# Gate and norm steps moved between VectorE, GpSimd and ScalarE, and the float16 half of the gelus moved to ScalarE, in a fused attention and expert kernel

## The reference

```python
# attention: 8 heads of 64, keys and values from the context and from x
x = x + tanh(g_xattn) * attention(layernorm(x), ctx, Wq1, Wk1, Wv1, Wk2, Wv2, Wo, bo)
# experts: 8 experts and a shared one, 128 -> 512 -> 128; two experts a token
logits = xf @ gate_w + gate_b
top_w, top_i = top_k(logits, 2)
gw = softmax(top_w)
combine = (gw[:, :, None] * one_hot(top_i, 8)).sum(axis=1)
for e in range(8):
    out += combine[:, e:e+1] * (gelu(xf @ w1[e] + b1[e]) @ w2[e] + b2[e])
shared = gelu(xf @ ws1 + bs1) @ ws2 + bs2
x = x + tanh(g_ffn) * (out + shared)
```

## Time and profile before

| | |
|---|---|
| median of 3 runs | 174.17 us (173.14 to 174.34) |
| profiled execution | 173.16 us |
| its span, first to last instruction | 171.0 us |
| mean granted clock of TensorE | 0.95 |
| busy: TensorE, VectorE, GpSimd, ScalarE | 144.5, 128.6, 123.9, 119.3 us |
| one undisturbed expert pass | 2.65 us |

### The profile page before, as it was taken

The page is one execution under the profiler, slowest core; times in us unless marked ns, Lnnn a source line. Parts: engine busy times, 40 slices in busy tenths (PEclk is TensorE's granted clock), DMA queues, the critical chain, the costliest instruction groups (busy, mean ns, idle before and its releaser), DMA issues.

```text
span 171.0 us, 4386 instructions
## 1 busy us (share of the span) xinstructions
PE 144.5 (84%) x1724; PEld 113.6 (66%) x1724; DVE 128.6 (75%) x267; ACT 119.3 (70%) x200; POOL 123.9 (72%) x98
## 2 busy tenths in 40 slices
PE   7789788568799989989997984999993599999973
PEld 4545334334578778767775873889992389999972
DVE  2779998647668868768698699877899955668681
ACT  3469663408989979889989896585964068787740
POOL 7639999619999999986879794836759355984430
PEclk9999999858999999999999997899999579999999
DMA  5599899970004701984000043000000000000002
GB/s 140 173 341 223 216 216 248 230 204 2 4 2 96 186 0 27 220 262 143 4 0 4 0 126 122 1 4 2 6 0 0 4 0 0 4 0 4 0 0 65
DMA packets 12925, 14.00 MB, mean 82 GB/s; under 512 B 1469, under 2 KB 9578, under 8 KB 12906
## 3 DMA queue, kind: packets, MB, share of 16 engines
q1 hardware_dynamic: 12906, 13.73, 30.4%
HBM read 7.18 MB, written 0.26 MB: 43 GB/s over the span
## 4 chain that ended last, share of the span: by engine, by line
PE 40%; DVE 30%; DMA 8%; POOL 6%; SPq 6%; issue 4%; ACT 3%; ACTq 0%; DVEq 0%
PE banks L951 8%; PE banks L952 8%; PE banks L953 8%; DVE nmax L783 4%; DVE v_lo L768 3%; DMA kab<-k_nat 3%; DMA ring<-in_L_ffn_w_dram 3%; PE banks L1051 2%; PE banks L1052 2%; SPq L452 2%; DVE wf L937 2%; PE banks L1032 2%; POOL p_lo L548 2%; DMA prob<-in_ctx_dram 2%; DVE kab L898 2%
## 5 line engine op out<-in xcount | busy, mean ns | idle before, releaser
L548 POOL TENSOR_TENSOR p_lo<-prob,p_hi 128x768 f16<-128x768 f32 x31 | 51.1, 1667 | 5.0 <-ACT p_hi L649 4.5
L783 DVE TENSOR_REDUCE nmax<-banks 128x1 f32<-128x768 f32 x32 | 30.5, 953 | 13.0 <-PE banks L1033 13.0
L587 POOL TENSOR_TENSOR kab<-kab 128x512 f16<-128x512 f32 x18 | 20.7, 1156 | 17.7 <-ACT kab L696 17.7
L641 ACT ACTIVATE prob<-banks 128x768 f32<-128x768 f32 x32 | 25.8, 805 | 9.1 <-PE banks L1052 8.1
L649 ACT ACTIVATE p_hi<-prob 128x768 f16<-128x768 f32 x32 | 27.0, 843 | 1.0
L690 ACT ACTIVATE kab<-banks,b1T 128x256 f32<-128x256 f32 x36 | 15.1, 471 | 17.5 <-PE banks L953 15.4
L951 PE MATMUL banks<-wf,kab 128*128 128x128 f16 x144 | 25.6, 222 | 1.0 <-DVE acc L929 0.9
L952 PE MATMUL banks<-wf,kab 128*128 128x128 f16 x144 | 25.6, 222 | 0.0
L953 PE MATMUL banks<-wf,kab 128*128 128x128 f16 x144 | 25.5, 222 | 0.0
L1052 PE MATMUL banks<-qab,kab 66*128 66x256 f16 x96 | 23.6, 278 | 0.0
L1051 PE MATMUL banks<-qab,kab 128*128 128x256 f16 x96 | 23.6, 278 | 0.0
(11 more groups left out here) (148 smaller groups left out, 392.1 us busy)
## 6 DMA issues: line engine op xcount, KB each, us to landing
ring<-in_L_ffn_w_dram SPq DMA_DIRECT2D x16, 256.0 KB, 3.9
kab<-k_nat SPq DMA_DIRECT2D x4, 384.0 KB, 4.6
kab<-k_nat SPq DMA_DIRECT2D x6, 192.0 KB, 4.5
kab<-k_nat SPq DMA_DIRECT2D x2, 576.0 KB, 7.1
qab<-qo SPq DMA_DIRECT2D x2, 384.0 KB, 6.3
kab<-k_nat SPq DMA_DIRECT2D x2, 288.0 KB, 8.0
prob<-in_ctx_dram SPq DMA_DIRECT2D x2, 256.0 KB, 4.7
ring<-in_L_xattn_Wk_dram SPq DMA_DIRECT2D x2, 256.0 KB, 4.2
```

The costliest lines, as they stand in the source:

```text
L548: nc.gpsimd.tensor_tensor(p_lo[:, j % 3, dst, :], prob(j, g)[:, 0:n, :], p_hi[:, j % 3, dst, :], ALU.subtract).then_inc(pl_done, 1)
L783: nc.vector.tensor_reduce(nmax[:, i, q:q + 1], span(0, KEYS), AX_X, ALU.max, negate=True).then_inc(max_done, 1)
```

## The change

There are four parts.

1. Norm: VectorE stops at mean and variance. GpSimd adds epsilon, takes the power, and makes -mean times rstd (`away`). ScalarE makes the normalised rows as one instruction of scale and bias a tile (`normal_rows`), in the step of TAIL_X; for batch 0 they stand between the two halves of the exponentials.
2. Gate: VectorE makes logits, largest values and marks, and the copy of the two largest is a reduction. GpSimd makes e to (logit - largest) for all eight experts, the mask and their product. VectorE sums it and takes the reciprocal. ScalarE multiplies (`combine`), as the last thing of its step.
3. Hidden chunks 2 and 3: their float16 copy goes from VectorE to ScalarE, behind the last gelu; both halves now count on `hh_act`.
4. Late weights: the low halves of experts 3 and 4 go from VectorE to GpSimd, and the steps are new for all of them. Also, VectorE makes the last `p_lo` at the start of its step.

```diff
-LO_BY_DVE = [3, 4]
-HI_STEP = {3: 13, 4: 14, 5: FFN0, 6: FFN0 + 3, 7: FFN0 + 6, 8: FFN0 + 9}
-LO_STEP = {3: 16, 4: 17, 5: FFN0 + 1, 6: FFN0 + 5, 7: FFN0 + 8, 8: FFN0 + 11}
+HI_STEP = {3: 13, 4: 14, 5: FFN0 + 1, 6: FFN0 + 4, 7: FFN0 + 7, 8: FFN0 + 10}
+SCALE_STEP = {3: FFN0, 4: FFN0 + 1, 5: FFN0 + 3, 6: FFN0 + 6, 7: FFN0 + 9, 8: FFN0 + 12}
+LO_STEP = {3: FFN0, 4: FFN0 + 2, 5: FFN0 + 4, 6: FFN0 + 7, 7: FFN0 + 10, 8: FFN0 + 13}
...
# GpSimd, in its steps
                         pool.wait_ge(var_ready, 2 + b)
-                        nc.gpsimd.tensor_tensor(rstd[:, t:t + QT], vare[:, t:t + QT], c_mhalf[:, t:t + QT],
-                                                ALU.pow).then_inc(rstd_ready, 1)
+                        link(nc.gpsimd.tensor_scalar(vare[:, t:t + QT], mv[:, t:t + QT, 1], EPS, None, ALU.add))
+                        link(nc.gpsimd.tensor_tensor(rstd[:, t:t + QT], vare[:, t:t + QT], c_mhalf[:, t:t + QT],
+                                                     ALU.pow))
+                        at = slice(QT * b, QT * b + QT)
+                        link(nc.gpsimd.tensor_scalar(away[:, 0, at], mv[:, t:t + QT, 0], -1.0, None, ALU.mult))
+                        nc.gpsimd.tensor_tensor(away[:, 1, at], away[:, 0, at], rstd[:, t:t + QT],
+                                                ALU.mult).then_inc(rstd_ready, 1)
                     if s == TAIL_GATE:
-                        pool.wait_ge(gexp_go, b + 1)
-                        nc.gpsimd.tensor_tensor(gexp[:, QT * b:QT * b + QT], c_e[:, :],
-                                                gdiff[:, QT * b:QT * b + QT], ALU.pow).then_inc(gexp_done, 1)
+                        at = slice(QT * b, QT * b + QT)
+                        pool.wait_ge(pick_done, b + 1)
+                        link(nc.gpsimd.tensor_tensor(gap[:, at, :], logit[:, at, 0:E],
+                                                     top8[:, at, 0:1].broadcast_to([P, QT, E]), ALU.subtract))
+                        link(nc.gpsimd.tensor_tensor(gap[:, at, :], c_e[:, :].unsqueeze(2).broadcast_to([P, QT, E]),
+                                                     gap[:, at, :], ALU.pow))
+                        link(nc.gpsimd.tensor_scalar(mask[:, at, :], marked[:, at, 0:E], PICKED, None, ALU.is_equal))
+                        nc.gpsimd.tensor_tensor(first[:, at, :], gap[:, at, :], mask[:, at, :],
+                                                ALU.mult).then_inc(gate_done, 1)
                 k = i - FFN0 - 1
                 if 0 <= k < NF:
-                    pool.wait_ge(hh_act, k + 1)
+                    pool.wait_ge(hh_act, 2 * k + 1)
...
                 for j in range(EARLY, NE):
-                    if j not in LO_BY_DVE and i == LO_STEP[j]:
+                    if i == SCALE_STEP[j]:
                         scale_late(j)
-                    if j not in LO_BY_DVE and i == LO_STEP[j] + 1:
+                    if i == LO_STEP[j]:
                         lo_late(j)
# ScalarE
+            def normal_rows(b):
+                act.wait_ge(rstd_ready, 2 + b)
+                for t in range(QT * b, QT * b + QT):
+                    nc.scalar.activation(xn[:, t, :], acc[:, t, :], ACT.Identity, bias=away[:, 1, t:t + 1],
+                                         scale=rstd[:, NT + t:NT + t + 1]).then_inc(xn_ready, 1)
+            def combine(b):
+                act.wait_ge(gate_sum, b + 1)
+                tiles = slice(QT * b, QT * b + QT)
+                for t in range(QT * b, QT * b + QT):
+                    nc.scalar.activation(comb[:, t, 0:E], first[:, t, :], ACT.Identity,
+                                         scale=gtop[:, t, 0:1]).then_inc(comb_part, 1)
+                act.wait_ge(comb_part, QT * (b + 1))
+                nc.scalar.activation(comb_s[:, tiles, :], comb[:, tiles, :], ACT.Identity,
+                                     scale=scales[:, 1:2]).then_inc(comb_ready, 1)
             for i in range(STEPS):
+                if i == TAIL_STEP[1][TAIL_X]:
+                    normal_rows(1)
...
+                if i == TAIL_STEP[0][TAIL_X]:
+                    normal_rows(0)
...
+                    act.wait_ge(gelu_done, HC * (k + 1))
+                    nc.scalar.activation(hid_hi[:, k % HB, HALF:], hid_b(k), ACT.Copy).then_inc(hh_act, 1)
+                for b in range(B):
+                    if i == TAIL_STEP[b][TAIL_COMB]:
+                        combine(b)
# VectorE, first in step 19 + k
-                    if k >= HB:
-                        dve.wait_ge(y_ps, k - HB + 1)
-                    dve.wait_ge(gelu_done, HC * (k + 1))
-                    nc.vector.tensor_copy(hid_hi[:, k % HB, HALF:], hid_b(k)).then_inc(hh_dve, 1)
-                    dve.wait_ge(hh_dve, k + 1)
+                    dve.wait_ge(hh_act, 2 * k + 2)
                     nc.vector.tensor_tensor(hid_lo[:, k % HB, HALF:], hid_b(k), hid_hi[:, k % HB, HALF:],
                                             ALU.subtract).then_inc(hl_dve, 1)
# VectorE, gate (TAIL_GATE, then TAIL_COMB); L855 to L864 and L809 to L819 are what goes
-                    mark(nc.vector.tensor_copy(pick8[:, tiles, 0:2], top8[:, tiles, 0:2]))
...
+                    link(nc.vector.tensor_reduce(pick8[:, tiles, 0:2], top8[:, tiles, 0:2].unsqueeze(3), AX_X, ALU.max))
...
+                    dve.wait_ge(gate_done, b + 1)
+                    link(nc.vector.tensor_reduce(gsum[:, tiles], first[:, tiles, :], AX_X, ALU.add))
+                    nc.vector.reciprocal(gtop[:, tiles, 0], gsum[:, tiles]).then_inc(gate_sum, 1)
# TensorE, before the hidden chunks of expert j for batch 0
-                        elif j in LO_BY_DVE:
-                            pe.wait_ge(f_lo_dve, LO_BY_DVE.index(j) + 1)
                         else:
-                            pe.wait_ge(f_lo_pool, j - EARLY - len(LO_BY_DVE) + 1)
+                            pe.wait_ge(f_lo, j - EARLY + 1)
```

More of the change, by code:

```diff
@@ L280, in block_kernel @@
         mask = sb("mask", [P, NT, E], F32)
+        gap = sb("gap", [P, NT, E], F32)
+        away = sb("away", [P, 2, NT], F32)
         first = sb("first", [P, NT, E], F32)
-        gdiff = sb("gdiff", [P, NT], F32)
-        gexp = sb("gexp", [P, NT], F32)
         gsum = sb("gsum", [P, NT], F32)
@@ L557, in lo_late @@
             def lo_late(j):
-                pool.wait_ge(f_scaled, j - EARLY + 1 - len(LO_BY_DVE))
+                pool.wait_ge(f_scaled, j - EARLY + 1)
                 hi, lo = [wf[:, a, EORDER[j], :, :].rearrange("p a n -> p (a n)") for a in range(2)]
                 nc.gpsimd.tensor_tensor(lo, ring_f(j).rearrange("p a n -> p (a n)"), hi,
-                                        ALU.subtract).then_inc(f_lo_pool, 1)
+                                        ALU.subtract).then_inc(f_lo, 1)
             for j in range(1, EARLY):
@@ L724, in row_statistics @@
                 for t in range(tiles):
-                    mark(nc.vector.bn_aggr(mv[:, first + t, :], stats[:, first + t, :]))
+                    last = nc.vector.bn_aggr(mv[:, first + t, :], stats[:, first + t, :])
+                    if first > 0 and t == tiles - 1:
+                        last.then_inc(var_ready, 1)
+                    else:
+                        mark(last)
                 settle()
+                if first > 0:
+                    return
                 nc.vector.tensor_scalar(vare[:, first:first + tiles], mv[:, first:first + tiles, 1], EPS, None,
@@ L803, in tail_first @@
                 tiles = slice(QT * b, QT * b + QT)
-                if s == TAIL_X:
-                    normalise_rows(acc[:, tiles, :], NT + QT * b, QT, 2 + b)
                 if s == TAIL_COMB:
[L808 to L821, removed]
+                    dve.wait_ge(gate_done, b + 1)
+                    link(nc.vector.tensor_reduce(gsum[:, tiles], first[:, tiles, :], AX_X, ALU.add))
+                    nc.vector.reciprocal(gtop[:, tiles, 0], gsum[:, tiles]).then_inc(gate_sum, 1)
             def tail(b, s):
@@ L854, in tail @@
                     settle()
-                    mark(nc.vector.tensor_copy(pick8[:, tiles, 0:2], top8[:, tiles, 0:2]))
[L856 to L860, removed]
+                    link(nc.vector.tensor_reduce(pick8[:, tiles, 0:2], top8[:, tiles, 0:2].unsqueeze(3), AX_X, ALU.max))
                     for t in range(QT * b, QT * b + QT):
-                        mark(nc.vector.match_replace(marked[:, t, :], pick8[:, t, :], logit[:, t, :], PICKED))
-                    settle()
-                    mark(nc.vector.tensor_scalar(mask[:, tiles, :], marked[:, tiles, 0:E], PICKED, None,
-                                                 ALU.is_equal))
+                        last = nc.vector.match_replace(marked[:, t, :], pick8[:, t, :], logit[:, t, :], PICKED)
+                        if t < QT * b + QT - 1:
+                            mark(last)
+                    last.then_inc(pick_done, 1)
                 elif s == TAIL_COMB:
@@ L913, in _ @@
                     shift_out(i - 1)
-                if i - HI_LAG == LO_LAST:
```

(12 more changed lines are left out.)

12 lines of the change are left out of this document (7 added, 5 removed).

## The result

The changed kernel is slower, 1.0253 times the kernel before, interval 1.0171 to 1.0335; the medians are 177.90 and 173.65 us (four runs each). In a second set of runs it was 1.0368 (1.0252 to 1.0485). The forecast was 176.5 us, from 171.0 to 178.8. The medians are of all executions, while the ratios leave out those in the chip's slower state, so that an experiment with too few others has no ratio.

A forecast was written before the change was run, and what follows sets the result against it. TensorE's work plus its gaps and half-clock stretches was taken as the bound. Terms -7.1 + 0.3 + 5.5 + 4.5 + 0.2 - 0.6 = +2.8 us gave 176.0 or 177.0, stated as 176.5 us, range 171.0 to 178.8.

The forecast's parts named there:

- The order on GpSimd behind the norm: Pass 5: expert 5's weights, queued behind batch 1's norm, ready at 124.6 us, wanted at 120.8; +5.5 us with 1.8 of clock.
- The power: Second gate, GpSimd: pow of 128x16 costs 0.165 us a column, 3.0 us for sixteen.
- the flat power: Rival at the second gate: pow takes 0.70 us at any width, total 174 to 175 us; chance 0.2.
- The low half of pass 5 behind the gate: Second gate, GpSimd: `lo` of pass 5 ready at 135.9 us, wanted at 133.0; gap 2.9, clock 1.6, +4.5 us.
- First gate: Batch 0's gate: its new end is ScalarE's `combine(0)`, at 105.4 to 106.0 us against 105.15; +0.3, from 0 to 1.7.
- the collision: First gate: VectorE's last `p_lo` meets GpSimd's gate on the shared port; up to 0.8 us later, left in the bound.
- One sign that I had named as against me: Sign of a wrong forecast: attention ending earlier than 100.9 us, if VectorE rather than ScalarE paced it.
- The pass: Expert passes: ScalarE with the added copy takes 2.58 us, under TensorE's 2.65, so passes stay at 2.65.
- The clock terms: Half-clock losses on TensorE after the gaps at pass 5 and its output half: 1.8 and 1.6 us.
- the sum: All terms together +2.8 us: 176.0 from the profiled run of 173.16 us, 177.0 from the median.
- The prize: Second gate of the kernel before: 5.0 us without matmul and 2.15 lost at half clock, 7.1 us to gain.

The follow-up runs named there:

- second profile: The changed kernel again, no edit: 1.0368 (1.0252 to 1.0485) times the kernel before, the profiled execution 179.69 us.

## Why the prediction was right, point by point

- **The order on GpSimd behind the norm.** Forecast: 7.7 us from the variances to expert 5, a gap of 3.7 us. Measured: 116.71 to 124.59, 7.9 us, gap 3.4. Late halves on VectorE took it away.
- **The power.** Forecast 3.0 us by the columns, 2.91 measured; the flat power falls.
- **The low half of pass 5 behind the gate.** Gap 2.9 forecast, 3.2 measured. Taking it ahead of the gate removed it.
- **First gate.** Forecast +0.3, from 0 to 1.7; measured 0.0. ScalarE does end it, as worked out, and the collision did not come: `p_lo` ran from 100.43 for 0.96 us, unhindered, beside the power. One sign that I had named as against me did come: ScalarE's last exponential half ended at 100.39 us, before 100.9 (it was 101.07). What made it 0.7 us sooner was not tested. TensorE reached the gate 1.7 us sooner and stood there until the weights came; this longer wait I had not foreseen.
- **The pass.** ScalarE starts its passes 2.58 us apart from 149.25 to 164.73 us, as forecast; TensorE's hidden chunks start 2.65 us apart in the changed kernel too. ScalarE's passes fit under TensorE's.
- **The clock terms failed as terms of one execution.** I put 1.8 and 1.6 us after two gaps. In the profiled execution no half-clock stretch followed either; in the second profile one followed both. As an average they may point the right way: five of the eight executions had a mean clock of 0.952 or less, where the profiled one had 0.98. But 177.27 and 178.52 us came at 0.981 and 0.979, so the clock does not explain those. That I took the kernel before's dips as certain was the error. Its clock row has further dips, at 30 to 43 us, which I did not read; the first gate came at the same time with a smaller one there.
- **A wait was missing.** I let pass 7's gelus go ahead and had `combine(1)` ready inside TensorE's output half. They wait 2.82 us for GpSimd's low half of pass 5, because they write its buffer (two buffers for three passes in flight), and TensorE waited 2.1 us more. In the profiled execution the two errors partly cancel: 3.4 us of clock not lost, 2.1 us of wait not foreseen. So the order on GpSimd was foreseen piece by piece, but that the sum, 176.0 from the profiled execution of before, comes so near 175.26 is in part luck.
- **The prize.** The 7.1 us of the earlier trace rows went as forecast in the profiled execution; in the second profile the half clock behind the second gate was there again. The kernel before with only TensorE's step moved shows that it can't be had by distance alone.
- **The cause beyond the forecast.** I named GpSimd's order as what eats the gain. With all of it mended the kernel was still 0.8% slower than before: the gate weights' place behind ScalarE's gelus, at both gates, eats it a second time, and both had to go for 3.1%.

## What to carry to other kernels

Moving work off a contended engine only pays if the new owner's queue is read from front to back: list what stands between its last wait and the result that the bounding engine asks for next, with a time for each. Where a small result is made behind the large work of the same step, let the consumer ask for it a step later; but check first what else queues behind it, as the same edit cost 1.5% where the producer was slow. And test the parts alone: they need not add up. Here they cost about 0, 0.7 and 4.7%, and all together 2.5 and 3.7% in two sets of runs.

## What the runs showed of the hardware

The granted clock after a gap is not a function of the gap's length alone. In one execution of the changed kernel gaps of 3.4, 3.2 and 2.1 us were followed by full clock, while one of 4.0 us before them was followed by 0.50; in another execution 0.50 followed gaps of 3.4 and 2.2 us. In the kernel before it followed the 2.4 us of the first gate:

```profile
106.00:107.00 1.00, 1.00 (x7) 0.50 0.83 253
```

GpSimd's power did not hold VectorE up as its subtraction did, beside which the same `p_lo` took 1.92 us. In the changed kernel VectorE's `p_lo`, with two SBUF inputs, took 0.96 us in the middle of it, and the power no longer than at the second gate, 2.91 us both times:

```profile
100.43 0.96 DVE L915 TENSOR_TENSOR p_lo<-prob,p_hi 128x768 f16<-128x768 f32 x1 [1.04 <-ACT p_hi L660]
```
```profile
99.15 2.91 POOL L590 TENSOR_TENSOR gap<-c_e,gap 128x16 f32<-128x16 f32 x1
```

The Trainium skill, SBUF — State Buffer, on the two separate sides, has the port that the two share locked for a whole instruction where VectorE has two SBUF inputs and GpSimd reads SBUF; by that `p_lo` would have waited until 102.06. It didn't, and the measurement decides. The other way round the rule fits: with norm and gate alone, the same power began while a VectorE weight half was running (99.29 for 1.22 us) and took 3.79 us, 0.88 more, where that half had 1.02 us to go.

```profile
99.49 3.79 POOL L590 TENSOR_TENSOR gap<-c_e,gap 128x16 f32<-128x16 f32 x1
```
